# The state's gate weights and the context of a recurrence in two f16 parts instead of three bf16 parts

## What is computed

```python
def step(carry, tgt):
    s, c, alpha = carry
    f = conv(alpha, conv_w)                                   # over 64 positions
    e = va . tanh(enc_proj + s @ Wa_s.T + f @ Wa_f + ba)      # scores
    alpha_new = softmax(where(mask, e, -1e30))
    g = alpha_new @ hbatch
    y = tanh(g @ L_gy_w.T + L_gy_b + s @ L_sy.T) @ L_yy_w.T + L_yy_b
    rec = tgt @ L_ys.T + s @ L_ss.T + g @ L_gs_w.T + L_gs_b
    ig, fg, cg, og = split(rec, 4)
    c_next = sig(fg) * c + sig(ig) * tanh(cg)
    s_next = sig(og) * tanh(c_next)
```

## Time and profile before

| | us |
|---|---|
| median of 3 runs | 1504.61 (1502.2 to 1511.74) |
| the profiled execution | 1507.64 |
| its span | 1505.8 |
| TensorE matmuls, busy | 1384.3 (92%) |
| VectorE, busy | 909.9 (60%) |
| ScalarE, busy | 586.7 (39%) |
| GpSimd, busy | 211.5 (14%) |
| mean granted clock | 0.94 |

### The profile page before, as it was taken

The page is one execution under the profiler, slowest core; times in us unless marked ns, Lnnn a source line. Parts: engine busy times, 40 slices in busy tenths (PEclk is TensorE's granted clock), DMA queues, the critical chain, the costliest instruction groups (busy, mean ns, idle before and its releaser), DMA issues.

```text
span 1505.8 us, 43803 instructions
## 1 busy us (share of the span) xinstructions
PE 1384.3 (92%) x17408; PEld 911.5 (61%) x17408; DVE 909.9 (60%) x4453; ACT 586.7 (39%) x2367; POOL 211.5 (14%) x704
## 2 busy tenths in 40 slices
PE   3566887999999999999999999999999999999988
PEld 1345665566665676766666665566665665666556
DVE  3664754366655666665666667666655666566643
ACT  3563662234333344333344434443333333333321
POOL 1001102011111111111111112221100011101111
PEclk8666897999999999999999999999989999899989
DMA  8462220000000000000000001200000000000000
GB/s 280 187 221 78 72 76 4 1 3 2 2 2 2 2 2 2 2 2 2 2 2 3 2 25 51 60 23 2 2 16 2 2 2 9 9 3 2 9 9 15
DMA packets 23874, 44.94 MB, mean 30 GB/s; under 512 B 8788, under 2 KB 12035, under 8 KB 23668
## 3 DMA queue, kind: packets, MB, share of 16 engines
q1 hardware_dynamic: 23668, 42.14, 8.6%
HBM read 40.04 MB, written 2.10 MB: 28 GB/s over the span
## 4 chain that ended last, share of the span: by engine, by line
PE 83%; DVE 7%; ACT 5%; issue 4%; SPq 1%; DMA 1%; POOL 0%; DVEq 0%; ACTq 0%; POOLq 0%
PE bank L1940 9%; PE bank L1861 9%; PE bank L1654 9%; PE bank L1883 8%; PE bank L1671 6%; PE bank L1915 6%; PE bank L1692 4%; PE bank L1889 4%; PE bank L1637 3%; PE bank L1897 3%; PE bank L1924 3%; PE bank L1903 2%; PE bank L1631 2%; PE bank L1539 2%; ACT interT L1217 2%
## 5 line engine op out<-in xcount | busy, mean ns | idle before, releaser
L1861 PE MATMUL bank<-ctx_lgs,identb 128*128 128x512 f16 (+2 forms) x685 | 191.8, 357 | 0.0
L1940 PE MATMUL bank<-ker_mem,uh 128*128 128x128 f32 x1020 | 184.0, 304 | 1.4 <-DVE ker_mem L1140 1.1
L1940 PEld LDWEIGHTS bank<-ker_mem,uh 128*128 128x128 f32 x1020 | 136.8, 194 | 67.4 <-DVE ker_mem L1140 50.1
L1654 PE MATMUL bank<-xT,wbig 128*128 128x256 f16 x1008 | 161.9, 274 | 0.0
L1459 ACT ACTIVATE xs<-gat 64x8 f32<-64x8 f32 x255 | 52.9, 207 | 245.6 <-DVE gat L1136 245.5
L1445 ACT ACTIVATE ker_mem<-bank 128x128 f16<-128x128 f32 x256 | 71.1, 278 | 185.5 <-PE bank L1883 185.5
L1450 ACT ACTIVATE eh<-bank,nmx 128x8 f16<-128x8 f32 x256 | 68.5, 268 | 173.6 <-PE bank L1906 173.6
L1671 PE MATMUL bank<-wbig,interT 128*128 128x512 f16 x378 | 124.3, 395 | 0.0
L1140 DVE TENSOR_TENSOR ker_mem<-inv,ahn 128x128 f32<-128x128 f32 x510 | 124.2, 285 | 0.0
L709 POOL TENSOR_TENSOR sscale<-ex,rinv 128x8 f32<-128x8 f32 x256 | 51.6, 201 | 505.5 <-DVE rinv L1125 505.5
L705 POOL COPY sscale<-s 64x4 f32<-64x4 f32 x256 | 59.5, 232 | 389.1 <-DVE s L1155 389.1
(11 more groups left out here) (234 smaller groups left out, 3191.2 us busy)
## 6 DMA issues: line engine op xcount, KB each, us to landing
kbd<-d_keys SPq DMA_DIRECT2D x32, 256.0 KB, 3.9
wbig<-d_gate_qT SPq DMA_DIRECT2D x4, 896.0 KB, 9.9
wbig<-d_up_qT SPq DMA_DIRECT2D x4, 896.0 KB, 20.7
wbig<-d_down_qT SPq DMA_DIRECT2D x1, 3584.0 KB, 13.2
sscale<-d_down_sT SPq DMA_DIRECT2D x4, 768.0 KB, 9.3
x_sb<-d_x SPq DMA_DIRECT2D x16, 128.0 KB, 3.0
d_out<-x_sb SPq DMA_DIRECT2D x16, 128.0 KB, 2.4
sscale<-d_gate_sT SPq DMA_DIRECT2D x2, 896.0 KB, 8.3
```

The source lines that it names most:

```text
L1654: last = mm(tile_bank(n)[:, lo:lo + QC], w[wi][:, kt, it * P:(it + 1) * P], x_part[q % 2][xi][:, kt, :], start=(kt == 0 and wi + xi == 0), ...
L1861: mm(bank[7][:, 0:n], identb[:], hg2[:, 0].rearrange("p h g -> p (h g)")[:, 0:n], start=True, stop=True)
L1940: mm(bank[0][:, 0:P], uh[:, h, :], qv[:, h, :, :], start=False, stop=False, skip_group_check=True)
```

## The change

The state's gate weights and the context part are held in two f16 parts in place of three bf16 parts. L1889 becomes six products for ten (weights high and low with `sh`, weights high with `sl`, for both halves of the gates), and the context part two matmuls for three. The setup uses `in_halves` for both, `in_parts` goes, and the identity for the context part and for the dummy matmuls is f16. The core of the diff:

```diff
@@ -110,13 +110,13 @@
-        identb = sb("identb", [P, P], BF16)
+        identh = sb("identh", [P, P], F16)
...
-        lss3 = sb("lss3", [J, 3, 256], BF16)
+        lss2 = sb("lss2", [J, 2, 256], F16)
...
-        enc3 = sb("enc3", [P, 3, P], BF16)
+        enc2 = sb("enc2", [P, 2, P], F16)
@@ -631,7 +631,7 @@
-            nc.gpsimd.tensor_copy(identb[:], ident[:]).then_inc(s["identb_ready"], 1)
+            nc.gpsimd.tensor_copy(identh[:], ident[:]).then_inc(s["identh_ready"], 1)
@@ -867,20 +867,13 @@
-            def in_parts(dst, src):
-
-                for j in range(2):
-                    link(nc.vector.tensor_copy(dst[:, j], src))
-                    link(nc.vector.tensor_tensor(src, src, dst[:, j], ALU.subtract))
-                nc.vector.tensor_copy(dst[:, 2], src).then_inc(s["part_ready"], 1)
...
-            in_parts(lss3[:], lssT[:])
+            in_halves(lss2[:], lssT[:])
...
-            in_parts(enc3[:], enc[:])
+            in_halves(enc2[:], enc[:])
@@ -1633,8 +1626,8 @@
             def context_part():
 
-                for j in range(3):
-                    mm(bank[0][:, 0:P], identb[:], enc3[:, j, :], start=(j == 0), stop=False, skip_group_check=True)
+                for j in range(2):
+                    mm(bank[0][:, 0:P], identh[:], enc2[:, j, :], start=(j == 0), stop=False, skip_group_check=True)
@@ -1858,7 +1851,7 @@
-                mm(bank[7][:, 0:n], identb[:], hg2[:, 0].rearrange("p h g -> p (h g)")[:, 0:n], start=True, stop=True)
+                mm(bank[7][:, 0:n], identh[:], hg2[:, 0].rearrange("p h g -> p (h g)")[:, 0:n], start=True, stop=True)
@@ -1885,9 +1878,9 @@
                 for gp in range(2):
-                    for j, st in ((0, sh), (1, sh), (2, sh), (0, sl), (1, sl)):
-                        last = mm(bank[2][:, 4 * gp:4 * gp + 4], lss3[:, j, gp * P:(gp + 1) * P], st[:],
-                                  start=(gp == 0 and j == 0 and st is sh), stop=(j == 1 and st is sl), skip_group_check=True)
+                    for j, st in ((0, sh), (1, sh), (0, sl)):
+                        last = mm(bank[2][:, 4 * gp:4 * gp + 4], lss2[:, j, gp * P:(gp + 1) * P], st[:],
+                                  start=(gp == 0 and j == 0 and st is sh), stop=(st is sl), skip_group_check=True)
                 last.then_inc(s["sp_done"], 1)
```

More of the change, by code:

```diff
@@ L271, in build @@
             prod_ready g_ready q0_ready q1_ready kept tg_ready ab_ready c_ready tc_ready s_ready sh_ready sl_ready sp_done
-            identb_ready hist_done part_ready
+            identh_ready hist_done part_ready
             split_high split_done gated upped stat_ready top_ready y_done u_ready yy_done lg_done lgx_ready pe_exp wsel_ready wt_done wT_ready wT_low_ready expert_ready""".split()
@@ L1626, in _ @@
             pe.wait_ge(s["part_ready"], 5)
-            pe.wait_ge(s["identb_ready"], 1)
+            pe.wait_ge(s["identh_ready"], 1)
             def masks():
```

## The result

The changed kernel takes 1494.22 us in the median of 9 runs (1489.18 to 1496.78), the kernel before 1505.61 beside it (9 runs, 1502.2 to 1518.46). The ratio is 0.9914, 95% interval 0.9897 to 0.993: 0.86% less. That is inside the bound of 1%, and clear of no change. The profiled execution has a span of 1492.3, 13.5 less than before.

What follows compares the result with a forecast made beforehand. TensorE's work ahead of L1897 was taken to bound the step, down to th_lo's floor. Gains of 7.9 and 5.0, given as 13.0 us, took the profiled 1507.64 to 1494.6; the median, 3.0 lower, gave 1491.6 us, range 1480 to 1504.

Steps and rivals of the forecast that it cites:

- The path: TensorE's work before L1897 sets the step; four of L1889's ten products fewer start the fill and L1897 0.10 us earlier.
- The floor: L1906 can't start before VectorE's th_lo (L1114) ends plus 0.06 us; all kinds of step go to 4.43 or 4.44.
- The price of 0.058 and 0.073 a step: Gain in us per step with a first fill of two 256-column matmuls and of one 512-column matmul, against 4.433.
- The counts: 137 steps at 0.058 and 69 at 0.073 gain 13.0 us; 42 with the 384-column dummy and about 7 more gain nothing.
- The context part at nothing: One 128-column context matmul fewer is hidden behind the reciprocal with 0.07 us to spare: 0, or 14 us without that cover.
- Rival C: TensorE's clock falls in more steps, 2.06 us each, eating the gain from seven steps on; 1510 us, chance 0.08.
- Setup: Before the loop, six VectorE operations fewer, hidden behind waits of 7.73 and 4.54 us: 0.
- rs: VectorE's rs (L1111) can start 0.10 us earlier, but only L1136 reads it, two microseconds later: 0.
- f16 for bf16: Type change in weights and the dummy's identity; a 0.005 us difference a step would be 1 us, taken as 0.

## Why the prediction was right, and what it left out

**The path.** Right, to a hundredth of a microsecond. The reading was that TensorE's fill and not ScalarE's tanh set L1897, from 0.17 between the two where 0.06 is enough. Four products more gave 0.10 a step and four fewer gave 0.06 to 0.07.

**The floor.** Right. L1906 was forecast at 1.35 and stands at 1.35 in all kinds; two further products fewer gave nothing, and a shorter th_lo gave 0.04. Read from the rows, the kind with 512 columns stands 0.09 above that floor and the kind with 384 columns 0.02, not the 0.08 and 0.01 of the working; the medians of the trace (1.434 and 1.365 before, 1.352 after) side with the working. The price of 0.058 and 0.073 a step was taken from the leanest steps, and the medians fell by 0.061 and 0.073. L1906 itself moved by 0.07; the 0.01 taken off for a weight load that has to wait was measured as 0.007 (behind L1906 the step takes 3.074 before and 3.081 after), and the load starts with its matmul where it was 0.08 ahead.

**The counts.** 13.0 forecast for the path; the two traces of the changed kernel give 14.1 and 13.7 at full clock. About right, and a little too small. The trace has 132 steps with a pair in the first fill and 73 with one matmul of 512, where the working took 137 and 69.

**The context part at nothing, for the step.** Right as far as the path goes: the reciprocal covers it, with the gates alone and with the context alone.

**The clock.** This is where the working was too coarse. It was made a rival with 0.08, as an event that would turn the gain into a loss, and against it stood that a lean stretch held its clock. It isn't all or nothing. The context half alone costs 0.4% (1.004), and the gates half alone has 0.9886; their product is 0.9925, and the whole change was measured at 0.9914 and 0.9944. So the term "context part: 0" should have been 0 for the step and some +6 us for the clock (0.4% of 1508). The sum had no term for the clock at all. Rival C's price was wrong too, in the other direction: some 2 us is what a step wholly at the lower level costs (step 75 of the changed kernel took 6.30), and most of the new low stretches touch two steps in part, such as 11 and 12, which took 5.16 and 4.66, 0.95 more together. By C's price the nine more such steps of the first profile would have eaten the gain; they cost some 2 us.

That the total came out to a tenth of a per cent is partly luck. In the profiled execution a path term 1 us too small and 1.6 us gained outside the loop, where executions differ by more than that (the loops of these traces begin between 282.9 and 289.6), made up for the 2 us of the clock. The gates half alone was worth 16 us (1508.27 less 1491.91) where 13 were forecast; its trace has 14.2 of them at full clock. In the second measurement of the whole change the gain was 0.56% (8.4 us), 4 to 5 less than forecast.

The Trainium skill (TensorE: Matmul & The Clock Gate, Part 1) has the throttled state as the default, released by activity. The runs here agree: thinner dummies 0.905, dummies in the gaps 0.939, at the same median step.

**Setup, rs, f16 for bf16.** The loop begins 0.3 us earlier, which is within what an execution varies. f16 weights went at the pace of bf16: the ten bf16 products started 0.025 apart and so do the six.

## What to carry to other kernels

To tell whether a few small instructions count, don't take either the chain or the waits for it: take two kinds of step that differ in one fill, compare when the next engine's instruction starts with the time that a release needs (here 0.06), and look for the next floor before multiplying. Work taken off an engine whose clock depends on being used isn't free where it was hidden: price each hidden cut also by what the clock does without it. Here the gates half alone, with the context part left as it was, was at least as good as the whole change. Dummies belong into gaps and not onto the path, but measure them: in the kernel before they gained nothing (0.9999), since 13 steps had no room for them.

## What was not expected of the hardware

- To take a matmul of 128 columns out of each 4.49 us, in a place where TensorE waits anyway (and to make the identity f16), cost 0.4% (1.004, 1.0022 to 1.0058), and its trace puts that down to the clock. No gap in TensorE's work was long: the longest idle time inside a common step was 0.09.
- With 256 for 512 columns in 124 dummies of one fill the changed kernel went from ratios of 0.9914 and 0.9944 to 1.0055, at a median step of 4.434; 1518.16 against the 1494.66 of the one with dummies in the gaps on the same chip.
- The lower clock comes back in the same steps: two profiles of the changed kernel have it in steps 11, 63, 72 to 76, 91 and 116.
- Run to run the time goes with the mean granted clock: in twelve runs of one kernel on one chip 1489.94 us at 0.937 and 1506.55 at 0.920, 17 us for 0.017.
- From the last of the products, on a tile of 64 rows, to the first matmul of the fill, on one of 128 rows, 0.09 passes (564.95 to 565.04 above), where equal ones start 0.025 apart. Where both sides have 128 rows the step from one line to the next took 0.03 (before, L1906 at 569.24 and the fill's L1730 at 569.27). That the tile is the cause no run isolates.
